# New orders for the four engines' lists of a layer kernel, one set each for the run-up, the steady bodies and the last four

## Chip, core and metric

One Trainium2 chip, one of its NeuronCores. The metric is the device time of one execution in microseconds (us), the median of the runs; lower is better.

## What is computed

Sixteen sequences of 512 tokens with 128 channels go through two layers. All arithmetic is float32 in meaning.

```python
x = x + chebyshev_attention(layernorm(x), W_in, W_out)       # 16 heads, causal running sums, orders 1 to 5
h = layernorm(x)                                             # the second layer normalises what it is given,
a = h + softmax_attention(layernorm(h) * g1 + b1)            # and normalises again inside: 16 heads of width 8, causal
a = a + moe(layernorm(a) * g2 + b2)                          # 8 experts of hidden width 512, top 2 for each token, erf gelu
return x + a
```

## The kernel before

The first phase is a software pipeline over the 16 sequences. `pipelined` (L327) calls `body` 21 times, with t from -5 to 15. Each body works on up to six sequences at once, each in another stage, and a stage whose sequence does not exist is None:

- f = t+5: first normalisation, projections, the Chebyshev powers of q and k;
- h = t+4: head sums, running sums, denominators, first output, residual, second pair of normalisations;
- g = t+3: projections of the softmax attention, the split of q and k into three bf16 parts, and their way through memory (`spread`) into the stack of rows that TensorE contracts over;
- m = t+2: for each query the maximum of its scores, in 44 tiles (`maximum`);
- b = t+1: scores again, with the maxima as two more rows of the stack, in 48 tiles (`scores`), exponentials (`exps`), values (`values`), normalisation of the output;
- t: second output, residual, third normalisation, gate, ranks, and `dispatch` of the tokens to the experts' regions by indirect DMAs.

So five bodies fill the pipeline (t = -5 to -1), twelve are full or nearly so (t = 0 to 11, with f None in the last), and four empty it (t = 12 to 15, where f and h are None and g runs in the first only). The second phase is the expert computation in 39 blocks and the sum of the pairs; neither its code nor its order is touched.

What sets the order: every engine takes its instructions strictly in the order in which the body issues them, and waits at its head for semaphores. For PE, DVE and ACT the body is a loop over 129 places, `for n in range(SLOTS)`; tables say at which places the many small tiles go (MAX_PE, SCORES_PE, VALUES_PE, MAX_DVE, EXPS_ACT, LEAVE_ACT), and `at(place, stage)` puts each other step at one place. One order serves all 21 bodies. POOL's body is plain code without places.

The steps that the prediction uses:

- `put_maxima(m, p, half)` (L974) issues on ACT's queue two DMAs of 8 KB that write the negated maxima of eight heads as two rows into the stack of scores of the coming body. `scores` number 0 of the next body waits for half 0 (`max_dma`, L1425 and after), number 24 for half 1.
- The stack reload (L392) is on SP's queue: two DMAs of 400 and 384 KB for each half of the heads. Half 0 may start once the spread is written and `scores` 24 of the body are done, half 1 once all 48 are done.
- `turn_maxima` (PE, L1406), `max_parts` (ACT, L972) and `max_rest` (DVE, L604) turn and split the maxima ahead of `put_maxima`.
- `turn_back`, `normalise`, `turn_y` and `take_y` (L994) end the body's attention; `output2` (PE, L1477) of the next body multiplies it, and `x2` (DVE, L621) adds the residual.
- `head_sums` (PE, L1320), ten matmuls each for k and q, need both powers of `fifth_order` (DVE, L536) and those of `even_orders` (POOL, L1153, L1154). `sum_k` (L553) and `den_terms` (L564) on DVE follow them.
- `ln_rsqrt` (POOL, L447 to L473) is a chain of small instructions; in its long form, for "m", it releases `apply1` and `apply2` (ACT, L480) and by them the next normalisation's turn.
- `less_first_part` (POOL, L1183) waits for the first bf16 parts that ACT writes in `take_qk` step 2 (L932, L934).
- `dispatch` (POOL, L1197) sends one tile of 128 tokens; there are eight for each sequence. For t = 12 to 14 it waits for the ones before, after each pair.

Of the kernel before, what the change touches and what calls it, by code (L numbers as in the profile page):

```python
# [28 lines left out]
B, T = 16, 512  # L29
QT = T // P  # L30
# [105 lines left out]
def block_kernel(nc, x, consts, cols, row_biases, w_in, w_out, wq, wk, wv, wp, gate_w, ew1, ew2, eb2, out):  # L136
    with ExitStack() as ctx:
# [87 lines left out]
        for c in "amb":  # L225
# [82 lines left out]
        SLOTS = 129  # L308

        MAX_PE = (0, 1, 5, 9, 12, 19, 21, 30, 31, 36, 44, 49, 51, 53, 56, 60, 62, 64, 67, 68, 70, 73, 75, 77, 81, 84, 86, 88, 91, 93,  # L310
                  95, 98, 100, 102, 106, 109, 112, 116, 118, 120, 121, 123, 124, 126)
        SCORES_PE = (2, 7, 8, 10, 11, 13, 14, 16, 17, 18, 20, 22, 24, 25, 27, 28, 32, 33, 35, 37, 40, 41, 46, 48, 50, 54, 55, 61, 66, 71,
                     72, 76, 82, 83, 87, 89, 92, 94, 97, 99, 104, 105, 108, 110, 111, 113, 115, 117)
        VALUES_PE = (15, 23, 26, 34, 43, 59, 78, 85, 101, 107, 119, 122)
        MAX_DVE = (1, 3, 5, 9, 11, 14, 15, 18, 23, 25, 27, 28, 29, 31, 32, 34, 35, 36, 38, 39, 40, 41, 44, 45, 49, 50, 53, 54, 56, 57,
                   58, 61, 62, 64, 66, 68, 69, 70, 71, 73, 74, 75, 76, 78)
        EXPS_ACT = (1, 3, 4, 5, 6, 7, 8, 9, 10, 11, 12, 13, 15, 16, 17, 18, 20, 21, 23, 24, 26, 28, 30, 35, 36, 39, 41, 44, 45, 49, 50,
                    52, 57, 59, 61, 62, 64, 65, 70, 71, 74, 76, 77, 78, 79, 80, 81, 82)
        LEAVE_ACT = (19, 42, 73)
        SPLIT_DVE, SPLIT_ACT = (8, 21, 52, 55), (0, 2, 32, 58, 60, 66, 72, 75)  # L320
# [15 lines left out]
        def _(sp):  # L336
# [28 lines left out]
            def body(t, b, m, g, h, f, p):  # L365
# [118 lines left out]
        def _(dve):  # L484
# [199 lines left out]
            def body(t, b, m, g, h, f, p):  # L684

                for n in range(SLOTS):
                    at = lambda place, stage: n == place and stage is not None
                    if b is None and t is not None and n in SPLIT_DVE:
                        second_weights(SPLIT_DVE.index(n))
                    if m is not None and n in MAX_DVE:  # L690
                        maximum(m, MAX_DVE.index(n))
                    if at(0, f):
                        stats0(f)
                        if f == 0:
                            set_tables()
                    if at(2, t):
                        x2(t)
                    if at(4, h):
                        sum_k(h)
                    if at(6, h):  # L700
                        den_terms(h)
                    if at(7, t):
                        stats3(t)
                    if at(10, h):
                        times_v(h, (0, 1))
                    if at(12, h):
                        sum_kv(h, (0,))
                    if at(13, h):
                        sum_kv(h, (1,))
                    if at(16, h):  # L710
                        times_v(h, (2, 3))
                    if at(17, h):
                        sum_kv(h, (2,))
                    if at(19, h):
                        times_v(h, (4,))
                    if at(20, h):
                        sum_kv(h, (3,))
                    if at(22, h):
                        sum_kv(h, (4,))
                    if at(24, h):  # L720
                        invert_den(h)
                    if at(26, t):
                        gate_top(t)
                    if at(30, t):
                        gate_weights(t)
                    if at(33, t):
                        slots(t)
                    if at(37, b):
                        normalise(b, 0)
                    if at(42, f):  # L730
                        clip(f, kx, W.hk_ev, W.k_clip)
                    if at(43, g):
                        third_part(g, 2, kf, ks)
                    if at(46, g):
                        third_part(g, 1, qf, qs)
                    if at(47, m):
                        max_rest(m, 0)
                    if at(48, f):
                        clip(f, qx, W.hq_ev, W.q_clip)
                    if at(51, f):  # L740
                        third_order(f, kx, W.k_sq, W.k_t35)
                    if at(59, b):
                        normalise(b, 1)
                    if at(60, h):
                        ratio(h)
                    if at(63, f):
                        third_order(f, qx, W.q_sq, W.q_t35)
                    if at(65, h):
                        add_x1(h)
                    if at(67, h):  # L750
                        stats1(h)
                    if at(72, b):
                        normalise(b, 2)
                    if at(77, b):
                        normalise(b, 3)
                    if at(79, f):
                        fifth_order(f, qx, W.q_sq, W.q_t35)
                    if at(80, f):
                        fifth_order(f, kx, W.k_sq, W.k_t35)
                    if at(81, m):  # L760
# [103 lines left out]
        def _(act):  # L864
# [151 lines left out]
            def body(t, b, m, g, h, f, p):  # L1016

                for n in range(SLOTS):
                    at = lambda place, stage: n == place and stage is not None
                    if b is None and t is not None and n in SPLIT_ACT:  # L1020
                        first_weights(SPLIT_ACT.index(n))
                    if b is not None and n in EXPS_ACT:
                        exps(b, EXPS_ACT.index(n))
                    if b is not None and n in LEAVE_ACT:
                        evacuate(b, LEAVE_ACT.index(n))
                    if at(14, t):
                        apply3(t)
                    if at(22, t):
                        affine2(t)
                    if at(25, f):  # L1030
# [616 lines left out]
```

## Time and profile before

| | us |
|---|---|
| median of 3 runs | 1379.57 (1373.16 to 1382.08) |
| the profiled execution | 1373.93 |
| its span, first to last instruction | 1372.1 |
| run-up, t = -5 to -1 | 0 to 210 |
| bodies t = 0 to 10 (eleven of them) | 210 to 836 |
| t = 11 to 15 | 836 to 1060 |
| experts and sum of pairs | 1060 to 1372 |

The borders are the times at which the first `scores` tile of a body starts, and for the second phase about the last dispatch. In the profile, "busy" is the time in which an engine ran instructions; PE's ends are modelled. "PEclk" is the granted clock of TensorE as a share of 2.4 GHz: 1.00 is 2.4 GHz and 0.50 is 1.2 GHz.

### The profile page before, as it was taken

Reading aid. Unit: us, or ns where it says so; the run is one execution under the profiler, and the core shown is the slowest. Engines: PE = TensorE matmul, PEld = TensorE weight load, DVE = VectorE, ACT = ScalarE, POOL = GpSimd, SP = SyncE. Lnnn points to the kernel's source line nnn. Section 1 sums busy time; section 2 is a strip of 40 time slices with the busy share of each in tenths; the row PEclk is TensorE's granted clock in tenths of the full one; section 3 lists DMA queues with packets and bytes.
Section 4 is the critical chain, followed back from the end, with each engine's and each line's share of the span. In section 5 each row is a group of like instructions: output and inputs, shape, how many; then the busy total and the mean of one; then the engine's idle time right before and its main releaser. Section 6 shows DMA issues by size and latency. Waiting matters only on the chain.

```text
span 1372.1 us, 27932 instructions
## 1 busy us (share of the span) xinstructions
PE 1141.6 (83%) x8883; PEld 702.2 (51%) x8883; DVE 1086.1 (79%) x2555; ACT 934.1 (68%) x1859; POOL 841.7 (61%) x1105
## 2 busy tenths in 40 slices
PE   3546898998989989889898998988893799999960
PEld 1223354454644546445464454544452588888840
DVE  4557888898988989899898897965715688888845
ACT  2334487696876968769687695675574699999940
POOL 2775566776877767777777686532224166666660
PEclk9677799999999999999999999988985899999985
DMA  9231231423324223142241422413232222222239
GB/s 207 50 88 51 49 88 30 109 72 60 97 51 105 72 58 101 31 115 78 58 103 41 96 77 44 104 62 73 84 127 104 78 79 85 84 86 82 67 139 367
DMA packets 84436, 121.91 MB, mean 89 GB/s; under 512 B 15270, under 2 KB 66522, under 8 KB 80002
## 3 DMA queue, kind: packets, MB, share of 16 engines
q1 hardware_dynamic: 70978, 98.07, 27.5%
q0 software_dynamic: 9088, 17.33, 3.6%
q10 hardware_dynamic: 4224, 4.72, 1.1%
q8 instruction: 71, 1.16, 0.4%
q14 instruction: 75, 0.61, 0.2%
HBM read 63.96 MB, written 57.46 MB: 88 GB/s over the span
## 4 chain that ended last, share of the span: by engine, by line
PE 65%; DMA 12%; DVE 10%; ACT 7%; issue 5%; POOL 1%; ACTq 1%; SPq 0%; POOLq 0%; DVEq 0%
PE back L1452 8%; PE front L1586 8%; PE back L1598 8%; DMA stack<-nms 7%; PE scores L1433 6%; PE front L1320 6%; PE maxima L1393 5%; ACT pr L986 4%; DVE nm L599 3%; PE scores L1435 3%; PE front L1295 3%; PE maxima L1395 3%; PE back L1270 2%; DMA stack<-pairs 2%; PE front L1477 1%
## 5 line engine op out<-in xcount | busy, mean ns | idle before, releaser
L986 ACT ACTIVATE pr<-scores 128x384 f32<-128x384 f32 (+1 forms) x768 | 369.6, 523 | 144.1 <-PE scores L1435 137.3
L599 DVE TENSOR_REDUCE nm<-maxima 128x1 f32<-128x384 f32 (+3 forms) x704 | 420.5, 631 | 44.4 <-PE maxima L1395 38.4
L1433 PE MATMUL scores<-stack 65*128 65x384 bf16 (+2 forms) x768 | 205.6, 285 | 57.3 <-DMA stack<-nms 32.6
L1393 PE MATMUL maxima<-stack 65*128 65x128 bf16 (+2 forms) x768 | 197.7, 282 | 16.2 <-DVE nm L599 14.5
L1197 POOL DMA_INDIRECT xg<-rows,sloti x128 | 137.0, 1070 | 108.0 <-DVE sloti L669 44.0
L1395 PE MATMUL maxima<-stack 128*128 128x128 bf16 x1024 | 182.6, 224 | 6.7 <-DMA stack<-spread 5.1
L1435 PE MATMUL scores<-stack 128*128 128x128 bf16 x1024 | 181.3, 225 | 0.0
L1452 PE MATMUL back<-pr,vaug 128*9 128x512 f32 (+3 forms) x2048 | 178.4, 444 | 1.5 <-ACT oT L990 1.0
L1433 PEld LDWEIGHTS scores<-stack 65*128 65x128 bf16 x768 | 75.6, 98 | 179.3 <-ACT pr L986 106.8
L1259 POOL DMA_INDIRECT pairs<-xs x104 | 111.0, 1068 | 78.7 <-DVE xs L832 51.9
L1393 PEld LDWEIGHTS maxima<-stack 65*128 65x128 bf16 x768 | 74.7, 98 | 121.9 <-DVE nm L599 87.4
L1586 PE MATMUL front<-h_first,w_now 128*128 128x512 f32 x312 | 126.2, 405 | 2.7 <-DVE h_second L812 2.5
L1127 ACT ACTIVATE xs<-front,b1p 128x512 f32<-128x512 f32 x156 | 107.5, 689 | 18.8 <-PE front L1586 16.6
L1162 POOL TENSOR_TENSOR kv<-F,kv 128x512 f32<-128x512 f32 x80 | 100.6, 1283 | 27.6 <-DVE kv L553 27.6
L1395 PEld LDWEIGHTS maxima<-stack 128*128 128x128 bf16 x1024 | 94.5, 100 | 29.9 <-issue 22.0
L1598 PE MATMUL back<-hid_first,w_now 128*128 128x512 f32 x312 | 96.3, 390 | 0.0
L1435 PEld LDWEIGHTS scores<-stack 128*128 128x128 bf16 x1024 | 92.4, 100 | 5.8 <-issue 4.6
L553 DVE TENSOR_TENSOR_SCAN kv<-one,front 128x512 f32<-128x512 f32 x80 | 93.7, 1204 | 0.0
L1320 PE MATMUL front<-F,cst 128*32 128x512 f32 x320 | 81.9, 804 | 3.9 <-DVE F L536 3.5
L1173 POOL TENSOR_TENSOR kv<-kv 128x512 f32<-128x512 f32 x64 | 80.4, 1267 | 2.4
L1153 POOL TENSOR_SCALAR F<-F 128x512 f32<-128x512 f32 x32 | 48.2, 1507 | 53.6 <-DVE F L532 53.3
L825 DVE TENSOR_TENSOR hid_second<-xs,hid_first 128x512 fp32r<-128x512 f32 x99 | 68.0, 687 | 15.7 <-ACT hid_first L1108 14.9
(219 smaller groups left out, 2459.5 us busy)
## 6 DMA issues: line engine op xcount, KB each, us to landing
stack<-spread SPq DMA_DIRECT2D x32, 400.0 KB
spread<-qs SPq DMA_DIRECT2D x96, 128.0 KB
spread<-ks SPq DMA_DIRECT2D x96, 128.0 KB
stack<-spread SPq DMA_DIRECT2D x32, 384.0 KB
xs<-xg SPq DMA_DIRECT2D x39, 272.0 KB, 2.9
stack<-pairs SPq DMA_DIRECT2D x8, 1024.0 KB, 13.5
stack<-in_consts SPq DMA_DIRECT2D x4, 1280.0 KB
xg<-xs SPq DMA_DIRECT2D x17, 272.0 KB
```

Of the source, the lines that this page charges most:

```text
L599: v.tensor_reduce(nm[:, h:h + heads, t], ring(n)[:, 0:heads * (t + 1) * P].rearrange("p (h n) -> p h n", h=heads), AX.X, ALU.max, negate=T ...
L986: a.activation(pr[:, n % PR, 0:width], ringE[n % 2][:, 0:width], ACT.Exp).then_inc(W.exp_ready, 1)
L1197: g_.indirect_dma_start(xg[:, :], bass.IndirectOffsetOnAxis(sloti[:, i, q:q + 1], 0), rows[:, i, q, :], None).then_inc(W.dispatched, 16)
L1259: g_.indirect_dma_start(pairs[:, :], bass.IndirectOffsetOnAxis(xt[i % XT][:, at:at + 1].bitcast(U32), 0), yo[i % 3][:, q * D:(q + 1) * D], ...
L1320: last = k.matmul(dst[32 * j:32 * j + 32, :], cst[:, C_SUM + 32 * var:C_SUM + 32 * var + 32], z[p], start=(p < 4), stop=(p > 0), skip_grou ...
L1393: k.matmul(ring(n)[:, at:at + t * P], qst[p][0:OPEN_ROWS, h, own], kst[p][0:OPEN_ROWS, h, 0:t * P], start=(j == 0), stop=True, skip_group_ ...
L1395: last = k.matmul(ring(n)[:, at + t * P:at + (t + 1) * P], qst[p][:, h, own], kst[p][:, h, own], start=(j == 0 and t == 0), stop=True, ski ...
L1433: k.matmul(dst[:, at + P:at + T - t * P], kst[p][0:OPEN_ROWS, h, own], qst[p][0:OPEN_ROWS, h, (t + 1) * P:T], start=(t == tiles[0]), stop= ...
L1435: last = k.matmul(dst[:, at:at + P], kst[p][:, h, own], qst[p][:, h, own], start=False, stop=True, skip_group_check=True)
L1452: last = k.matmul(V[32 * i:32 * i + DH + 1, t * P:T], vaug[:, b % VR, t, 4 * (s_ // 3) + i, :], pr[:, (4 * s_ + i) % PR, at:at + T - t * P ...
L1586: last = k.matmul((X, Y)[n % 2][:, :], w_now[:, i % 2, wi, c * P:(c + 1) * P], h2p[hi][:, i % 2, :], start=(j == 0), stop=(j == len(TERMS3 ...
L1598: last = k.matmul((Z, V)[i % 2][:, :], w_now[:, i % 2, 2 + wi, c * P:(c + 1) * P], (hidh, hidl)[hi][i % 2 * HC + c], start=(c == 0 and j = ...
```

## The change

Each step's single place becomes three, one each for the run-up, the steady bodies and the last four, and `body` is given `w` to choose. POOL gets a list of 25 places. One wait is added: `turn_ln` now waits also for `x2`, which reads the same PSUM bank.

```diff
 for t in range(-5, B):
-    body(*(t + i if 0 <= t + i < B else None for i in range(6)), (t + 1) % 2)
+    body(*(...), (t + 1) % 2, (t >= 0) + (t >= 12))

 # every body
-    at = lambda place, stage: n == place and stage is not None
+    at = lambda places, stage: n == places[w] and stage is not None

 # ACT
-if at(83, m):
+if at((77, 75, 70), m):
     put_maxima(m, p, 0)
-if at(38, g):
+if at((39, 41, 43), g):
     take_qk(g, 2)
-if at(22, t):
+if at((18, 16, 20), t):
     affine2(t)
-if at(34, t):
+if at((8, 36, 30), t):
     gate_exp(t)
 # unmoved in the steady bodies: put_maxima(m, p, 1) at 88, apply2 at 89

 # PE
-if at(4, h): head_sums(h, kx, ...)
-if at(6, h): head_sums(h, qx, ...)
+if at((0, 4, 66), h): head_sums(h, kx, ...)
+if at((2, 5, 17), h): head_sums(h, qx, ...)
-if at(47, g): project_k2(g)
-if at(52, g): project_q2(g, h)
+if at((47, 50, 59), g): project_q2(g, h)
+if at((41, 55, 44), g): project_k2(g)
-if at(58, t): ranks(t)
+if at((37, 60, 50), t): ranks(t)
-if at(127, b): turn_y(b)
-if at(128, m): turn_maxima(m, b, 1)
+if at((128, 127, 128), m): turn_maxima(m, b, 1)
+if at((127, 128, 127), b): turn_y(b)
-MAX_PE = (0, 1, 5, 9, 12, ...)
-SCORES_PE = (2, 7, 8, 10, 11, 13, ...)
+MAX_PE = ((6, 12, 14, ...), (1, 2, 12, 20, ...), (1, 2, 4, 7, ...))
+SCORES_PE = ((1, 3, 4, ...), (0, 6, 7, 8, 9, ...), (0, 6, 8, 9, ...))

 # DVE
-if at(0, f): stats0(f)
-if at(2, t): x2(t)
-if at(4, h): sum_k(h)
-if at(6, h): den_terms(h)
-if at(7, t): stats3(t)
+if at((68, 2, 3), t): x2(t)
+if at((81, 3, 5), t): stats3(t)
+if at((1, 4, 81), h): sum_k(h)
+if at((0, 5, 7), f): stats0(f)
+if at((2, 7, 15), h): den_terms(h)
-if at(46, g): third_part(g, 1, qf, qs)
+if at((47, 51, 60), g): third_part(g, 1, qf, qs)
-if at(80, f): fifth_order(f, kx, ...)
+if at((51, 80, 19), f): fifth_order(f, kx, ...)
-MAX_DVE = (1, 3, 5, 9, ...)
+MAX_DVE = ((8, 9, 10, ...), (0, 1, 12, 13, ...), (0, 2, 4, ...))

 # POOL, steady bodies: before
-add_residual, ln_rsqrt b, times_q 0, ln_rsqrt a, times_q 1 to 4, add_products (0, 1), less_first_part 0, 1,
-add_products (2, 3), dispatch x3, even_orders k, dispatch x3, even_orders q, ln_rsqrt m, dispatch x2, keep_residual
 # and after
+ln_rsqrt b, add_residual, ln_rsqrt a, times_q 0 to 4, add_products (0, 1), less_first_part 0, add_products (2, 3),
+less_first_part 1, dispatch x6, even_orders k, dispatch x2, even_orders q, ln_rsqrt m, keep_residual

 # PE
-def turn_ln(g, h):
+def turn_ln(g, h, t):
     pe.wait_ge(norm["m"]["out"], g * 8 + 8)
+    if t is not None:
+        pe.wait_ge(W.x2_ready, t + 1)
```

`SPLIT_DVE` and `SPLIT_ACT`, the places in body t = 15 at which the experts' weights are split, move from (8, 21, 52, 55) and (0, 2, 32, ...) to (20, 36, 45, 52) and (17, 24, 58, ...). The other places change by a few, as in the lines above.

## Rows read from the trace of the kernel before

**Rows 1.** The page: busy time, share of the span and instructions of each engine.

```profile
PE 1141.6 (83%) x8883; PEld 702.2 (51%) x8883; DVE 1086.1 (79%) x2555; ACT 934.1 (68%) x1859; POOL 841.7 (61%) x1105
```

**Rows 2.** Windows by body: length, busy (count) of PE, PEld, DVE, ACT, POOL; PEclk, DMA share, GB/s.

```profile
382.00:437.00 55.00, 50.66 (x473) 28.74 (x473) 50.79 (x130) 43.01 (x93) 42.85 (x59) 1.00 0.33 79
...
552.00:611.00 59.00, 53.93 (x475) 29.95 (x476) 51.68 (x130) 43.60 (x95) 43.07 (x60) 0.95 0.31 74
```

**Rows 3.** The chain that ended last, at the border into t = 6: start, us, what.

```profile
544.85 7.17 DMA stack<-nms
552.07 0.50 PE scores L1433
...
552.67 1.81 PE front L1477 x8
554.49 3.55 PE front L1320 x10
...
558.37 1.83 PE front L1320 x10
```

**Rows 4.** Timeline of PE at the border into t = 3: start, us, instruction [idle before <-releaser].

```profile
381.99 0.34 PE L1433 MATMUL scores<-stack 65*128 65x384 bf16 x1 [2.27 <-DMA stack<-nms]
...
385.43 1.90 PE L1320 MATMUL front<-F,cst 128*32 128x512 f32 x10
```

**Rows 5.** Waits in the eleven steady bodies: total us, times, longest.

```profile
PE scores L1433 <- DMA stack<-nms: 24.4, 11, 2.7
```

**Rows 6.** Timeline of ACT at the border into t = 6 and near the end of t = 6.

```profile
549.82 0.57 ACT L994 ACTIVATE hn<-back 128x512 f32<-128x512 f32 x1
...
552.20 1.65 ACT L480 ACTIVATE ha<-xs,morem 128x128 f32<-128x128 f32 x4 [1.80 <-POOL morem L473]
553.75 0.57 ACT L986 ACTIVATE pr<-scores 128x512 f32<-128x512 f32 x1
...
599.99 2.97 ACT L986 ACTIVATE pr<-scores 128x384 f32<-128x384 f32 x6 [0.78 <-PE scores L1435]
```

**Rows 7.** Windows of 1 us at the end of t = 6: ACT busy, PEclk, DMA share, GB/s.

```profile
600.00:601.00 1.00, 0.97 (x3) 1.00 0.04 13
...
605.00:606.00 1.00, 0.77 (x2) 1.00 1.38 239
```

**Rows 8.** DMA issues: KB each and median us from issue to landing.

```profile
gw_sb<-in_gate_w SPq DMA_DIRECT2D x1, 4.0 KB, 2.0
```

**Rows 9.** Timeline of POOL through t = 6.

```profile
544.07 0.22 POOL L447 TENSOR_SCALAR lnvm<-mvm 128x4 f32<-128x4 f32 x1
...
551.97 0.20 POOL L473 TENSOR_TENSOR morem<-morem 128x4 f32<-128x4 f32 x1
...
581.02 1.17 POOL L1183 TENSOR_TENSOR qf<-qf,qs 128x512 f32<-128x512 f32 x1 [1.62 <-ACT qs L932]
...
592.26 1.51 POOL L1153 TENSOR_SCALAR F<-F 128x512 f32<-128x512 f32 x1 [1.52 <-DVE F L532]
...
596.78 0.96 POOL L1197 DMA_INDIRECT xg<-rows,sloti  x1 [0.30 <-issue]
...
602.06 0.22 POOL L447 TENSOR_SCALAR lnvm<-mvm 128x4 f32<-128x4 f32 x1
```

**Rows 10.** Timeline of DVE and PE in the run-up, into t = -3 and t = -2.

```profile
56.97 0.69 DVE L584 TENSOR_TENSOR xs<-front,xs 128x512 f32<-128x512 f32 x1 [1.57 <-PE front L1355]
...
59.03 1.26 DVE L536 SCALAR_TENSOR_TENSOR F<-F 128x512 f32<-128x512 f32 x2
...
60.44 6.54 PE L1320 MATMUL front<-F,cst 128*32 128x512 f32 x20 [3.51 <-DVE F L536]
...
102.26 3.62 PE L1320 MATMUL front<-F,cst 128*32 128x512 f32 x10
```

**Rows 11.** Timelines of ACT and POOL in t = 14.

```profile
1013.28 0.20 ACT L1003 ACTIVATE gt<-gt 128x4 f32<-128x4 f32 x1
...
1016.97 1.10 POOL L1197 DMA_INDIRECT xg<-rows,sloti  x1 [16.38 <-DVE sloti L669]
```

More of the change, by code:

```diff
@@ L738, in body @@
[L738 to L742, printed above, removed]
[L743 to L748 removed]
+                    if at((39, 43, 53), g):
+                        third_part(g, 2, kf, ks)
@@ new lines, in body @@
+            def body(t, b, m, g, h, f, p, w):
+                for n in range(POOL_SLOTS):
+                    at = lambda places, stage: n == places[w] and stage is not None
+                    if at((20, 0, 3), t):
+                        ln_rsqrt("b", t)
+                    if at((1, 1, 2), t):
+                        add_residual(t)
+                    if at((2, 2, 22), f):
+                        ln_rsqrt("a", f)
+                    if at((3, 3, 9), h):
+                        times_q(h, (0,))
+                    if at((5, 4, 21), h):
+                        times_q(h, (1,))
+                    if at((8, 5, 13), h):
+                        times_q(h, (2,))
+                    if at((10, 6, 6), h):
+                        times_q(h, (3,))
+                    if at((15, 7, 7), h):
+                        times_q(h, (4,))
+                    if at((14, 8, 23), h):
+                        add_products(h, (0, 1))
+                    if at((11, 9, 5), g):
+                        less_first_part(g, 0)
+                    if at((17, 10, 14), h):
+                        add_products(h, (2, 3))
+                    if at((13, 11, 8), g):
+                        less_first_part(g, 1)
+                    if at((4, 12, 4), t):
+                        dispatch(t, 0, (0,))
+                    if at((7, 13, 10), t):
+                        dispatch(t, 0, (1,))
+                    if at((6, 14, 11), t):
+                        dispatch(t, 0, (2,))
+                    if at((24, 15, 12), t):
+                        dispatch(t, 0, (3,))
+                    if at((0, 16, 15), t):
+                        dispatch(t, 1, (0,))
+                    if at((9, 17, 16), t):
+                        dispatch(t, 1, (1,))
+                    if at((19, 18, 1), f):
+                        even_orders(f, kx, W.k_t35, W.k_t24)
+                    if at((16, 19, 18), t):
+                        dispatch(t, 1, (2,))
+                    if at((12, 20, 19), t):
+                        dispatch(t, 1, (3,))
+                    if at((21, 21, 17), f):
+                        even_orders(f, qx, W.q_t35, W.q_t24)
+                    if at((22, 22, 20), h):
+                        ln_rsqrt("m", h)
+                    if at((23, 23, 0), h):
+                        keep_residual(h)
+                    if at((18, 24, 24), t):
+                        wait_apart(pool, W.dispatched, t * (16 * 2 * QT) + 16 * 2 * QT)
+                        pool.sem_inc(W.rows_free, 1)
```

314 lines of the change are left out of this document (141 added, 173 removed), and 20 rows, old and new, of tables (EXPS_ACT, MAX_DVE, MAX_PE, SCORES_PE).

## The prediction

> **What bounds the kernel now.** I read the page first, for shares: PE is busy 83% of the span, DVE 79%, ACT 68%, POOL 61% [rows 1]. No engine stands out, so the average says little. Cutting the span into bodies says more. A steady body is DVE 51 to 52 us busy and PE 50 to 54, in 55 to 59 us [rows 2]. Two engines are near full, and what is left over is 4 to 7 us in each body. The reader should also see PEclk there: 1.00 in the 55 us body, 0.95 in the 59 us one. Of the twelve bodies from t = 0, three look like the first and nine like the second.
>
> Then the chain of waits, to see where those microseconds lie. At each border between bodies it leaves the engines: 7.17 us of DMA, the rows of the maxima of half 0, and only then the first scores tile of the new body [rows 3]. The waits confirm it: in eleven bodies PE stood 24.4 us before that tile, 2.2 each time [rows 5]. PE is in order, so the second output and the head sums, which need none of these rows, stand behind the tile. What follows runs slow as well: 3.55 us for ten head-sum matmuls that take 1.83 a few microseconds later, and 1.81 for the second output [rows 3]. Where the clock stays up, the whole set is over 5.34 us after the wait (381.99 to 387.33) against 8.13 in the slow case (552.07 to 560.20) [rows 3, 4].
>
> What releases the DMA late: it is issued behind the last exponential of the body, in the moment in which SP issues the reload of half 1. The DMA engines have nothing to do just before, a share of 0.04 at 600 us, and are flooded at 605 [rows 7].
>
> **The change, part by part, for a steady body.**
>
> *The rows of the maxima earlier (ACT place 83 to 75).* Seven exponentials now come behind them instead of none. The last six take 2.97 us from 599.99 [rows 6], so the issue moves some 4 us ahead, to about 599, into the gap of the DMA engines [rows 7]. How long they take alone no row shows: the nearest below is 2.0 us for a 4 KB load [rows 8], above 7.17 beside the reload [rows 3]. I take 3, near the small load, since the gap is empty: landed at 602. Even with 7.17 they land at 606, two microseconds before PE wants them at about 608, so this term holds over the whole bound. Price on ACT: two issues, some 1.1 us, now between two exponentials. The 0.78 us in which ACT waits for PE there [rows 6] hide most of it. Taken at nothing; without that cover it is 1.1 x 12 = 13 us.
>
> *What is late next at the border.* The second output needs take_y, which ended at 550.39 [rows 6]. From there: second output 0.95, two scores and maxima tiles 0.4, head sums 2 x 1.83 at the full clock, so done at 555.4 instead of 560.2, 4.8 us earlier. By the same sum at the fast border 2.2 earlier. Over twelve borders 9 x 4.8 + 3 x 2.2 = 50 us, if nothing takes it back.
>
> *POOL takes some back.* Its list closes a loop. The long ln_rsqrt of h ends at 552.17 and releases apply2 and then the first exponential at 553.75 [rows 6, 9]. From there the body runs on to the first bf16 parts at 581.02, which is 28.9 us, and POOL's list from there to the start of the next ln_rsqrt takes 21.0 (to 602.06) and that one 8.1 (544.07 to 552.17) [rows 9]: 58.0 in all. After the change two dispatches (0.96 + 0.30 each [rows 9]) stand before ln_rsqrt instead of behind it, +2.5, and the wait of 1.5 us before even_orders goes, because six dispatches instead of three stand before it: 22.1 + 8.1 = 30.2. On the other side of the loop the 4.8 us of the border come off. But project_k2, which the parts need, moves from PE place 47 (and q from 52) to 55, with two more scores tiles and one more maximum ahead; at half a microsecond of exponential each (2.97 for six [rows 6]) that is +1. So the slow body becomes 58.0 + 1.0 + 1.0 - 4.8 = 55.2, the fast one about 54.8 by the same steps. The 1.0 on POOL lies on the path only in part, because keep_residual and add_residual no longer stand ahead of the norms, so I take 54 for all. The floor is DVE's 51.2 busy [rows 2]; with the 5% of gaps that it has in the middle of a body that is 53.
>
> *The clock.* At nine borders the granted clock went from its 2.4 GHz level to 1.2 GHz after PE's idle wait, and three times, with the same wait, it did not [rows 2 to 4]. The sum above has it stay up. The Trainium skill (TensorE: Matmul & The Clock Gate, "What's actually happening") says that the slow clock is the default and activity lifts it. By that rule a filled border keeps the fast one. The trace agrees as far as the full-clock middles of the bodies go; no row shows a filled border. Should it fall anyway, the price is 3.55 - 1.83 and 1.81 - 0.95, 2.6 us at each of nine borders.
>
> *x2's wait added to turn_ln.* In the steady bodies x2 is done some 20 us before; nothing.
>
> So 56.9 us a body (626 us for eleven) become 54: 12 x 2.9 = 35 us.
>
> **The run-up.** Head sums of k started at 60.44, released by fifth_order at 59.03, itself behind the statistics; the bank was free from x1 at 57.66 [rows 10]. The new place of fifth_order for k, 51 instead of 80, removes that: 2.7 us into t = -3. Into t = -2 the maxima stood ahead of the head sums and held them to 102.26 [rows 10]; they now come behind. By the same distance to x1 the sums start some 4.7 us earlier. These bodies are then bound by other things, DVE above all, so of the 7.4 and of the border into t = -1 I take 6, with 0 and 14 as ends.
>
> **The last four.** The borders into t = 13 and 14 have the same DMA wait with the slow clock behind it, 2 us and 1 to 2 us of slow matmuls: I take 3 each, 6. In t = 14 the gate's exponential at 1013.28 leads to the dispatch at 1016.97, for which POOL had waited 16.4 us [rows 11]; it now has 18 exponentials ahead instead of 23, 5 x 0.5 = 2.5, and ranks come eight places sooner. I take 4. The weight splits move behind the third normalisation of t = 15 and cost ACT 2.6 us that end before the second phase needs them: nothing. The second phase stays.
>
> **Sum.** 35 + 6 + 6 + 4 = 51 from the profiled execution's 1373.9: 1323. The median of the runs is 5.6 us above that execution and two of three are near the median. On its scale it is 1328; I say 1326.
>
> **Rivals.**
> - *The wait goes, half of the gain stays away.* The clock falls at the border all the same, 9 x 2.6 = 23, or POOL's loop stays at its full 55.2 (+14), with some of both at the ends: 1326 + 25 = 1351. For it: nine of twelve borders fell, and the gap before turn_y stays. Against: three did not fall even with 2.3 us of idling.
> - *The maxima land no earlier where it counts.* third_part of q moves from place 46 to 51 and less_first_part of k behind two additions, so the reload of half 0 slides into the 600 us gap and the rows arrive beside it, and this repeats at every border. Then only run-up and tail change: 1372 (-8). Against: 7.17 us from 599 is still in time.
> - *Slower: POOL's loop takes over.* This happens if the border's gain does not reach the bf16 parts, since the first exponential waits for apply2, so for POOL, while POOL's own part has grown from 29.1 to 30.2. The loop is slower than the 56.9 of now once the way from ln_rsqrt's end to the parts takes over 26.7 us; it took 28.9 in the slow body and I count on 25. At 28 it is 58.2, +1.3 x 12 = 16, and the last bodies inherit it: 1398. Against: in the old order head sums, not apply2, held the second exponential back by 6 us.
>
> **How the numbers follow.** Forecast 0.65, first rival 0.20, second 0.07, slower 0.08. The forecast's own range is 1300 (bodies of 53, run-up 12, tail 12) to 1345 (ACT's issues uncovered). The range with the first rival in it is 1296 to 1358. A per cent, 14 us, is about what this kernel's measurement can tell. The forecast and the first rival lie beyond it on the fast side: faster 0.84, same 0.08, slower 0.08.
>
> **What would show it.** In the profile after: no DMA step of the maxima in the chain at steady borders; PE's wait for them under 0.5 us each; steady bodies of about 54 us at PEclk 1.00, DVE 94 to 95% busy; head sums into t = -2 before the first maxima. Wrong: bodies above 56 with PEclk below 0.98, or POOL idle under 5 us a body with ACT waiting for L473.

## The result, and the profile after

The changed kernel takes 1336.4 us, median of four executions (1332.6 to 1343.8), beside 1379.0 us for the kernel before on the same chip: a ratio of 0.971, with a 95% interval of 0.966 to 0.975. The forecast was 1326, the range 1296 to 1358. The gain is 43 us where 53 were forecast, on the side that had been given 0.84.

The profiled execution of the changed kernel is the slowest of its four (1343.8 us, span 1342.0). The one of before was 5.6 us under its median. So the two traces differ by only 30 us, and what follows uses them for where the time lies, and the medians for how much it is. One execution of the kernel before on another chip (chip B below) took 2715.6 us and is left out everywhere.

The page's first part, with the same columns as [rows 1]:

```profile
PE 1131.7 (84%) x8883; PEld 706.3 (53%) x8883; DVE 1101.1 (82%) x2555; ACT 938.9 (70%) x1859; POOL 845.8 (63%) x1105
```

The counts are the same, so the instructions are the same and only their order moved. DVE's busy time still rose by 15 us; the section on the prediction comes back to that. Windows by body, with the columns of [rows 2]:

```profile
264.00:320.00 56.00, 52.65 (x465) 29.78 (x466) 51.16 (x128) 42.94 (x92) 42.07 (x60) 0.94 0.28 72
377.00:431.00 54.00, 50.37 (x474) 28.87 (x473) 51.52 (x129) 43.46 (x93) 42.57 (x60) 1.00 0.33 81
...
541.00:596.00 55.00, 51.04 (x478) 29.36 (x477) 52.48 (x130) 43.54 (x93) 42.29 (x60) 1.00 0.34 80
```

DVE is now busy for 51.2 to 52.5 us in 54 to 56. The granted clock is 1.00 in two of the three windows shown; over the eleven bodies t = 0 to 10 of this trace it is 1.00 in six and 0.94 to 0.97 in the others. Before, nine bodies of twelve fell [rows 2].

The border into t = 5 in PE's timeline. It corresponds to [rows 4], where PE stood 2.27 us for the maxima's rows:

```profile
484.42 0.22 PE L1430 MATMUL maxima<-stack 128*128 128x128 bf16 x1
484.84 1.16 PE L1512 MATMUL front<-wp_sb,hn 128*128 128x128 f32 x8 [0.21 <-ACT hn L1014]
485.93 3.62 PE L1353 MATMUL front<-F,cst 128*32 128x512 f32 x20
489.64 0.34 PE L1468 MATMUL scores<-stack 65*128 65x384 bf16 x1
```

The second output (L1512) and the twenty head sums (L1353) run at the full clock, without the wait, and before the first scores tile. In the list of waits the step "scores <- DMA stack<-nms" of [rows 5] (24.4 us) no longer occurs. The rows land in 3.3 us (all instructions on that tile, so both halves, last line of the answer; 208 to 820 us; half 0 alone 3.1 to 4.3):

```profile
DMA to landing us min/median/max: 1.9/3.3/4.3
```

What is late next stands in the chain of waits, here the end of t = 5 (start, us, what):

```profile
522.43 0.96 POOL xg L1217
523.70 0.95 POOL xg L1217
...
525.95 1.55 POOL F L1173
527.50 1.46 POOL F L1174
...
534.91 1.05 POOL lnvm L468
538.14 0.67 ACT hs L500 x2
...
539.94 0.49 ACT hn L1014
540.47 1.16 PE front L1512 x8
541.63 3.55 PE front L1353 x20
```

This end of the chain goes through POOL: its gathers (`xg`, the indirect DMAs of `dispatch`), even_orders, the norm's reciprocal root, then ACT and the head sums. That is POOL's loop from the prediction. POOL's waits over the steady bodies (208 to 819 us: total us, times, longest):

```profile
POOL qf L1203 <- ACT qs L952: 38.7, 11, 3.8
...
POOL xg L1217 <- ACT rows L1027: 14.7, 10, 3.1
```

The second line is new: POOL's gathers wait for ACT's copy of the rows, which moved from ACT place 29 to 49. ACT's waits in the same stretch:

```profile
ACT pr L1006 <- PE scores L1470: 48.4, 84, 1.7
ACT ha L500 <- POOL morem L493: 25.2, 11, 2.7
```

The last view is ACT's timeline at the new place of the first issue:

```profile
584.12 0.53 ACTq L997 DMA_DIRECT2D stack<-nms  x1
584.44 0.48 ACT L1006 ACTIVATE pr<-scores 128x384 f32<-128x384 f32 x1
584.68 1.93 ACTq L997 DMA_DIRECT2D stack<-nms  x1
586.72 2.41 ACT L1006 ACTIVATE pr<-scores 128x384 f32<-128x384 f32 x5 [1.79 <-issue]
```

The second of the two issues takes 1.93 us here, and the next exponential starts as it ends (584.68 + 1.93 = 586.61), after 1.79 us of idle time. This is the longest of eleven such places: the second issue of half 0 takes 0.95 to 1.93 us in them, with a median of 1.22, and ACT is idle for 0.81 to 1.79 us, with a median of 1.08.

Where the microseconds went is read from one mark per body, the start of the head sums of k. The first column is its time in t = -1, the second the twelve bodies from there to the mark in t = 11 (so t = -1 and the eleven steady bodies t = 0 to 10), the third what remains to the end of the span (the steady body t = 11, the last four and the second phase). The experiments of the next section stand in the same table. A to D are the chips on which the kernels ran, and the ratio is against the kernel before on the same chip.

| kernel | chip | to t = -1 | 12 bodies | rest | span | ratio |
|---|---|---|---|---|---|---|
| before | A | 155.3 | 683.1 | 533.7 | 1372.1 | 1 |
| changed | A | 151.2 | 667.7 | 523.1 | 1342.0 | 0.971 |
| before (c0_before) | B | 158.4 | 689.2 | 534.2 | 1381.7 | 1 |
| changed (c1_after) | B | 151.6 | 662.5 | 525.1 | 1339.2 | 0.972 |
| e5_steady_before | B | 151.4 | 659.5 | 523.9 | 1334.8 | 0.965 |
| e6_only_steady_new | B | 155.1 | 660.8 | 540.6 | 1356.5 | 0.983 |
| e1_put_early | C | 157.7 | 667.6 | 545.2 | 1370.5 | 0.968 |
| e2_put_late | C | 145.7 | 792.4 | 555.5 | 1493.6 | 1.051 |
| e3_copy_early | C | 151.3 | 711.8 | 543.9 | 1407.0 | 0.999 |
| e4_pool_before | C | 146.3 | 741.2 | 542.5 | 1430.0 | 1.018 |
| changed (c2_after) | D | 151.5 | 714.7 | 545.8 | 1412.0 | 0.998 |
| e7_put_early_again | D | 156.2 | 664.3 | 548.4 | 1368.9 | 0.972 |
| e8_copy_early_again | D | 151.2 | 711.8 | 540.9 | 1404.0 | 1.003 |
| e9_pool_before_again | D | 147.0 | 744.9 | 549.1 | 1441.0 | 1.020 |

On chip A the change wins 4 us before t = -1, 15 in the twelve bodies and 11 in the rest. On chip B both traces lie within 3 us of their medians, and there it is 7, 27 and 9, together 42.5, the whole gain. So the pair of B is the better guide to sizes. Over t = 0 to 10 alone a body goes from 56.9 us to 55.5 on A and from 57.5 to 55.0 on B. The second phase is untouched: from its first matmul to the end it takes 298.7 us before (from 1073.4) and 298.9 after (from 1043.1).

### The profile page after: what moved, and what is told of

Read it like the earlier page. It is cut to its first block, busy times and chain, and to the rows that moved or that the text cites. A ratio compares the mean times of both kernels' runs of the same rounds, so it can differ in the third digit from the quotient of the medians.

```text
span 1342.0 us, 27933 instructions
## 1 busy us (share of the span) xinstructions
PE 1131.7 (84%) x8883; PEld 706.3 (53%) x8883; DVE 1101.1 (82%) x2555; ACT 938.9 (70%) x1859; POOL 845.8 (63%) x1105
## 3 DMA queue, kind: packets, MB, share of 16 engines
q8 instruction: 71, 1.16, 0.4%
## 4 chain that ended last, share of the span: by engine, by line
PE 49%; DVE 17%; POOL 12%; issue 9%; ACT 8%; DMA 4%; POOLq 1%; ACTq 0%; SPq 0%; DVEq 0%
PE front L1621 8%; PE back L1633 8%; DVE nm L619 7%; PE back L1487 5%; POOL xg L1217 4%; PE scores L1468 4%; PE front L1353 4%; ACT pr L1006 3%; PE maxima L1428 3%; POOL F L1173 2%; PE scores L1470 2%; DMA stack<-pairs 2%; DVE front L570 2%; POOL F L1174 2%; PE maxima L1430 2%
## 5 line engine op out<-in xcount | busy, mean ns | idle before, releaser
L1006 ACT ACTIVATE pr<-scores 128x384 f32<-128x384 f32 (+1 forms) x768 | 373.5, 524 | 105.6 <-PE scores L1470 88.3
L1217 POOL DMA_INDIRECT xg<-rows,sloti x128 | 133.0, 1039 | 130.0 <-ACT rows L1027 43.4
L1182 POOL TENSOR_TENSOR kv<-F,kv 128x512 f32<-128x512 f32 x80 | 107.9, 1372 | 21.8 <-DVE kv L573 21.8
L1147 ACT ACTIVATE xs<-front,b1p 128x512 f32<-128x512 f32 x156 | 107.7, 690 | 18.6 <-PE front L1621 16.6
L1128 ACT ACTIVATE hid_first<-xs 128x512 fp32r<-128x512 f32 x117 | 74.1, 634 | 3.7
L1292 POOL DMA_INDIRECT pairs<-pr,xs x52 | 55.0, 1058 | 26.9 <-DVE pr L852 12.3
```

The costliest lines, as they stand in the source:

```text
L1006: a.activation(pr[:, n % PR, 0:width], ringE[n % 2][:, 0:width], ACT.Exp).then_inc(W.exp_ready, 1)
L1182: g_.tensor_tensor(kv[:, p, :], qx[p], kv[:, p, :], ALU.mult).then_inc(W.qk_prod, 1)
L1217: g_.indirect_dma_start(xg[:, :], bass.IndirectOffsetOnAxis(sloti[:, i, q:q + 1], 0), rows[:, i, q, :], None).then_inc(W.dispatched, 16)
L1292: g_.indirect_dma_start(pairs[:, :], bass.IndirectOffsetOnAxis(xt[i % XT][:, at:at + 1].bitcast(U32), 0), yo[i % 3][:, q * D:(q + 1) * D], ...
```

## The experiments

The theory: the first issue of the maxima's rows, moved ahead of the reload of half 1, is what gains in the steady bodies; the run-up and the last four gain a little of their own; POOL's loop takes the rest back. The rival: the new orders as a whole carry the gain, and the issue alone does little.

**e1_put_early, e7_put_early_again.** The kernel before with one number changed:

```diff
-                    if at(83, m):
+                    if at(75, m):
                         put_maxima(m, p, 0)
```

> The kernel before with one edit: the rows of the maxima of half 0 are issued at ACT place 75 instead of 83, in all bodies. If the gain is the wait at the border between bodies, PE's wait for these rows goes and most of the 42.6 us of the whole change comes with this edit alone: 1341 to 1356. If the new orders carry the gain and the early rows only permit it, this stays within 8 us of the kernel before: 1371 or more.

It took 1371.0 us beside 1415.9 for the kernel before: ratio 0.968 (0.965 to 0.971). Chip C was slower than chip A with the kernel before, so it was run again, on a fourth chip:

> The same kernel as the experiment with the early issue alone (the kernel before, with only the first issue of the maxima's rows moved from place 83 to 75), because that ran on a chip on which the kernel before took 1416 us. Theory (the early issue is the gain of the steady bodies; the rest of the change's gain is run-up and last four): about 1380 - 26 = 1354 us where before takes 1380, which lies between the kernel before and the changed one (1340). Rival (it is worth the whole change, as its ratio of 0.968 on the other chip says): 1337 us or less.

1372.2 beside 1409.5, ratio 0.972 (0.966 to 0.977). The microseconds of both my sentences were worked out for a chip on which before takes 1380, so they can't be held against this run. The ratio can: 0.972 of 1380 is 1341, nearer the rival's 1337 than the theory's 1354. On chips C and D the one moved issue is worth as much as the whole change is on A. This compares times alone, since the kernel before was not traced on C or D; e5 below makes the same comparison in traces of one chip. The twelve bodies of e7 are 55.4 us each (664.3 / 12), with PE and DVE busy for 93% of the stretch:

```profile
208.00:811.00 603.00, 560.15 (x5137) 313.91 (x5135) 558.40 (x1401) 470.48 (x1013) 462.48 (x633) 0.99 0.31 77
```

**e2_put_late.** The changed kernel with the issue back behind the last exponentials, all other orders new:

```diff
-                    if at((77, 75, 70), m):
+                    if at((83, 83, 82), m):
                         put_maxima(m, p, 0)
```

> The kernel after with the rows of half 0 issued behind the last exponentials again (places 83, 83, 82); all else stays. Border theory: PE waits 2 us and more for the rows at each of fourteen borders, with slow clock behind most, 1360 to 1380. If the orders carry it: under 1345. The two issues no longer stand between exponentials 40 and 41, where ACT idled 0.8 to 1.8 us, so if that is on the path some 1 us a body comes back, inside these numbers.

1489.1 us, ratio to before 1.051 (1.047 to 1.054), far more than the expected 1360 to 1380, even counting that chip C is slower; the changed kernel took 0.998 of before on chip D. D is close to C in every kernel that ran on both (before 1415.9 and 1409.5, the others 1371.0 and 1372.2, 1414.8 and 1415.0, 1438.1 and 1442.9 us). So the place of this issue is worth about 5% within the new orders, 78 us in the twelve bodies (792.4 against 714.7, on two chips). PE's waits in the steady bodies are back, and longer than in [rows 5]:

```profile
PE scores L1468 <- DMA stack<-nms: 33.0, 9, 3.8
```

and behind each of them the second output runs at half the speed, as in [rows 3] (PE's timeline at a border):

```profile
397.57 0.50 PE L1468 MATMUL scores<-stack 65*128 65x384 bf16 x1 [3.60 <-DMA stack<-nms]
...
398.83 2.02 PE L1512 MATMUL front<-wp_sb,hn 128*128 128x128 f32 x8
```

**e3_copy_early, e8_copy_early_again.** The changed kernel with ACT's copy of the rows back at its old place in the steady bodies. I had not priced this move in the prediction, and POOL's new wait of 14.7 us made it a suspect.

```diff
-                    if at((28, 49, 36), t):
+                    if at((28, 29, 36), t):
                         copy_rows(t)
```

> The kernel after with copy_rows at ACT place 29 instead of 49 in the steady bodies, as in the kernel before. In the trace after, POOL stands 14.7 us in eleven steady bodies before its first dispatch for copy_rows. If POOL's loop is what sets the body now, nearly all of it comes back: 1.0 to 1.3 us a body, 1321 to 1326. If DVE or the loop through the exponentials sets the body, nothing: 1333 to 1340.

1414.8 us, ratio 0.999 (0.997 to 1.002), which looks like a loss of 3% against the changed kernel of chip A. It isn't one; that took a second run beside the changed kernel:

> The same kernel as the copy_rows experiment (changed kernel, ACT copies the rows at place 29 again in the steady bodies). Theory: POOL's wait of 14 us for the rows goes, and turns into as much waiting of POOL for DVE's F tiles, so it equals the changed kernel within 5 us, and its 1415 us were the chip's: stalls of ACT and DVE that the trace put down to nothing in the kernel ('remote', 35 us together) and that the changed kernel's second trace doesn't have. Rival (the edit itself upsets ACT's list): 30 us or more slower than the changed kernel, with the same bodies of 58 to 62 us.

1415.0 us beside 1409.2 for the changed kernel (c2_after) on the same chip. Ratios to before 1.003 (1.000 to 1.006) and 0.998 (0.996 to 1.001): within half a per cent, a shade slower if anything. POOL's wait for the rows is gone and its wait for F is up from 32.5 us in the changed kernel on that chip to

```profile
POOL F L1173 <- DVE F L552: 47.8, 17, 4.0
```

So the suspect is cleared, on these chips; on A and B the edit was not tried. What POOL doesn't wait for at the gathers, it waits for at even_orders behind them. The 3% belong to the chip and the changed kernel together, as c2_after below shows.

**e4_pool_before, e9_pool_before_again.** The changed kernel with POOL's list of before in the steady bodies, the other three engines' lists new:

```diff
             def body(t, b, m, g, h, f, p, w):
+                if w == 1:
+                    if t is not None:
+                        add_residual(t)
+                        ln_rsqrt("b", t)
...
+                    return
                 for n in range(POOL_SLOTS):
```

> The kernel after with POOL's order of the kernel before in the steady bodies. My prediction priced the new order of POOL at about +1 us a body (two dispatches ahead of the long norm chain, less one wait): by that this kernel is 5 to 12 us faster, 1325 to 1331. If the early third normalisation and the order around less_first_part pay for more than that, it is slower: 1342 to 1355.

1438.1 us, 1.018 (1.014 to 1.022), and again with the changed kernel beside it:

> The same kernel as the experiment with POOL's order of before in the steady bodies beside the other three engines' new orders. Theory: POOL's old order puts the even orders of k after three gathers only, and copying the rows now comes late, so POOL waits for ACT's rows and DVE for F: steady bodies longer by 2 to 4 us, 1365 to 1390 us. Rival (only the slow chip made it 1438): equal to the changed kernel within 5 us.

1442.9 us against 1409.2: 2.4% slower, 30 us in the twelve bodies (744.9 against 714.7), 2.5 each, within the 2 to 4 expected. (The 1365 to 1390 us were worked out for a chip like A.) The changed kernel carries a stall of some 2.4 us in most of its bodies on this chip, described under c2_after, and e9 does not have it in t = 0 to 10, so the old list costs more than these 2.5 us. ACT's apply3 now waits 39.3 us for POOL's norm of t, which stands behind add_residual again, and POOL waits for DVE:

```profile
ACT rows L500 <- POOL moreb L491: 39.3, 9, 4.7
...
POOL F L1173 <- DVE F L552: 35.2, 10, 5.3
POOL kv L1182 <- DVE kv L573: 29.1, 19, 2.3
```

The lists belong together. POOL's new one is worth nothing by itself that I could show, but the other three don't run with the old one.

**c0_before and c1_after.** Both kernels unchanged, to learn what chip C does; they ran on chip B.

> The kernel before, unchanged, looked at on the chip that ran the first four experiments, where it took 1415.94 us against 1379 on the other one. If that chip is slower evenly, every steady body is some 2.7% longer (58.4 us instead of 56.9) with the same waits; if its DMA transfers or its instruction supply are slower, the difference sits in one kind of wait: landings of the maxima's rows above 7.2 us, or idle time that the trace puts down to nothing ('issue', 'remote').

> The changed kernel, unchanged, on the chip of the experiments. If the chip is slower by one factor, it takes 1336 x 1415.9 / 1379 = 1372 us, ratio 0.970; then copying the rows at place 29 cost 3% (42 us) and POOL's old order in the steady bodies 4.8% (66 us). Rival: the changed kernel suffers more from whatever slows this chip, as the 57.6 to 62.4 us bodies of the copy_rows experiment suggest: then it takes 1400 to 1415 here, and those two edits cost little or nothing.

Chip B is like chip A (before 1381.3; this execution 1383.6). The changed kernel took 1340.7, ratio 0.972 (0.965 to 0.978): the result of chip A again. What it would do on chip C, the actual question, stayed open; on D, which is close to C, the rival's 1400 to 1415 us came (c2_after). The profile of before on chip B repeats its wait, 24.4 us in all, and gives a number that [rows 3] could only show once, the landing of half 0 issued in the same moment as the reload:

```profile
DMA to landing us min/median/max: 5.9/6.8/8.0
```

**e5_steady_before.** The changed kernel, with all four lists of before in the twelve steady bodies and only the issue moved in them; run-up and last four as changed. The edit is the one of e4 for all four engines, with this in ACT's copy of the old list:

```diff
-                        if at(83, m):
+                        if at(75, m):
                             put_maxima(m, p, 0)
```

> The changed kernel with all four engines' orders of before in the twelve steady bodies, and only the first issue of the maxima's rows moved to place 75 in them; run-up and last four as changed. Theory (the early issue is the whole gain of the steady bodies, the new steady orders add nothing): steady bodies of 55.0 us as in the experiment with that one edit (1371 us), the run-up shorter by about 6 and the last four by about 8: 1357 us, ratio 0.958, not slower than the changed kernel. Rival (the new steady orders are worth their part, and the one edit alone only had luck on its chip): slower than the changed kernel on this chip by 10 us or more.

1330.7 us (1328.6 to 1336.7) beside 1340.7 (1335.1 to 1343.6) for the changed kernel on the same chip; ratios 0.965 (0.959 to 0.970) and 0.972 (0.965 to 0.978). The rival is out: the new steady orders gain nothing that the issue doesn't give alone. The theory's side, not slower, holds; by the medians it is 10 us faster, with intervals that overlap. (Its 1357 us were worked out from e1's time on the slower chip.) Within the steady bodies e5 differs from the kernel before by this one issue and by the wait added to turn_ln, and against c0_before on the same chip the twelve bodies gain 29.7 us (689.2 and 659.5), where the new lists gain 26.7. It is the fastest kernel of this study. The rows of half 0 land sooner:

```profile
DMA to landing us min/median/max: 1.9/2.2/3.2
```

The reload of half 0 is issued about 6 us before these rows in e5 and 4.0 us before them in the changed kernel, that of half 1 some 4 and 5.5 us behind them. In the microsecond of the first issue the DMA share is 0.39 to 0.61 in the eleven bodies of e5 and 0.78 to 1.14 in those of the changed kernel. The second issue takes 0.61 us in eight of e5's eleven bodies. That this is worth the 10 us is not shown.

**e6_only_steady_new.** The reverse: new lists in the steady bodies, the old ones, with the issue at place 83, in run-up and last four.

```diff
             def body(t, b, m, g, h, f, p, w):
+                if w != 1:
...
+                        if at(83, m):
+                            put_maxima(m, p, 0)
...
+                    return
```

> The changed kernel with the orders of before in the run-up and the last four bodies (the maxima's first rows at place 83 there), the new orders only in the twelve steady bodies. Theory: run-up and last four are worth about 4 and 11 us of the 43, so this is 15 us slower than the changed kernel (about 1387 us here, ratio 0.98). Rival: the stages gain nothing of their own (what the run-up wins is given back at its end), and it equals the changed kernel within 5 us.

1358.4 us, 17.7 slower than the changed kernel, where the theory said 15. By the table, 3.5 of it lie before t = -1 and 15.5 behind the mark in t = 11, more than the 9 to 11 that this part gains against the kernel before. That the old last bodies fit the new steady ones less well than their own would explain it; it was not tested.

**c2_after.** The changed kernel beside e7, e8 and e9, on chip D.

> The changed kernel once more, so that the other three of this call are compared on one chip. On a chip on which before takes 1380: 1340 us. On the one on which it takes 1416: 1372 if that chip slows all kernels alike, 1400 or more if it slows the changed one more; the first would leave the copy_rows and POOL experiments' losses as costs of their edits.

1409.2 us, ratio to before 0.998 (0.996 to 1.001). Here the change gains nothing, while one edit of it gains 2.8% (e7). Of the two cases in that sentence the second came: the chip slows the changed kernel more than the one before. So the losses of e3 and e4 against 0.971 are not the cost of their edits alone, as read above. The time is in the steady bodies, 59.7 us each (t = 0 to 10) against 55.0 on B, and a stall stands in nine of these eleven. ACT's timeline on chip B, then on chip D, at the same instructions:

```profile
299.16 0.63 ACT L917 ACTIVATE F<-F 128x512 f32<-128x512 f32 x1 [0.33 <-DVE F L547]
299.80 0.49 ACT L1006 ACTIVATE pr<-scores 128x384 f32<-128x384 f32 x1
300.18 0.71 ACT L922 ACTIVATE F<-F,negc 128x512 f32<-128x512 f32 x1
```

```profile
299.92 0.63 ACT L917 ACTIVATE F<-F 128x512 f32<-128x512 f32 x1 [0.29 <-issue]
302.99 0.49 ACT L1006 ACTIVATE pr<-scores 128x384 f32<-128x384 f32 x1 [2.44 <-remote]
303.38 0.71 ACT L922 ACTIVATE F<-F,negc 128x512 f32<-128x512 f32 x1
```

From 297 us to this point the two traces run 0.76 us apart, instruction by instruction. Then ACT stands 2.44 us, ended by nothing that the profile knows ("remote"), and DVE waits 1.15 us for a maximum of PE in the same stretch. The stall comes again at 363.78, 422.98, 483.42, 542.10, 602.70, 661.90, 722.35 and 842.78, always at this instruction, always of 2.44 to 2.49 us; the body around 782 us has none. So the stall itself makes some 22 of the 52 us that the twelve bodies are longer than on B. Some 5 us behind the first one PE's clock is down (windows of 1 us, PE alone: busy, PEclk, DMA share, GB/s):

```profile
302.00:303.00 1.00, 0.81 (x2) 1.00 0.20 70
303.00:304.00 1.00, 0.46 (x8) 1.00 0.05 17
...
307.00:308.00 1.00, 1.00 (x9) 1.00 0.62 115
308.00:309.00 1.00, 0.87 (x6) 0.75 0.90 279
309.00:310.00 1.00, 1.00 (x8) 0.50 1.19 180
```

On B the same windows are full and stay at 1.00. On D the clock stays at 0.50, its 1.2 GHz level, for some seven microseconds behind the thinned stretch (300 to 307 us), in which PE was busy for 0.44 to 0.81 of each microsecond.

Which kernels have the stall? On C and D those with POOL's new steady list do: e2, e3, e8 and c2_after show 6 to 9 of 2 us and more in t = 0 to 10, on ACT in front of an exponential, up to 4.1 us long. Those with the old list (e1, e7, e4, e9) show none there; e1 and e7 have only 0.8 us or less on DVE, at xs, in most bodies. On A and B no kernel has it. The new list puts six of POOL's gathers in a row across this stretch, the old one three.

One body separates the gathers from the rest of the list. In t = 11 there is no f, so the old list skips even_orders too, and six gathers stand in a row there as well. In just that body e1 has two stalls of 2 us and more on ACT (2.65 and 2.17 us) and so has e4 (2.91 and 2.44). The last of the six gathers and the two stalls, from e1:

```profile
862.74 0.96 POOL L1197 DMA_INDIRECT xg<-rows,sloti  x1 [0.30 <-issue]
```

```profile
860.50 0.27 ACT L972 ACTIVATE nms<-maxima 32x128 bf16<-32x128 f32 x1 [2.65 <-remote]
...
864.92 1.10 ACT L986 ACTIVATE pr<-scores 128x384 f32<-128x384 f32 x2 [2.17 <-remote]
```

That makes the six gathers in a row the strong candidate. It is still argued, not shown: of the other kernels on C and D only e3 has the stall on ACT in t = 11, though all have the six gathers there; no run changed the gathers alone, and what on the chip holds ACT back was not found. Nor was e5 tried on C or D.

## Why the prediction was right, and where it was not

**The border (4.8 us at slow ones, 2.2 at fast ones).** Right in its mechanism. The DMA step is gone from the waits, the head sums run as one set of 3.55 to 3.62 us, and the clock holds. e5 shows on one chip that this one issue gives the gain of the steady bodies, e1 and e7 agree, and e2 shows that taking it back costs more than all the change gained. The sum took 0.95 us for the second output at the full clock; it takes 1.11 to 1.16.

**The rows' landing (3 us taken, between 2.0 and 7.17).** 3.3 measured, 2.2 in e5. The size is right, but not for the reason given, that the gap is empty: in the changed kernel the reload of half 0 is issued 4.0 us before the rows, and the DMA share is 0.97 in the microsecond of the first issue at 584 us. The rows landed in time all the same. That the size came out so near is luck.

**The two issues on ACT (taken at nothing; 13 us if uncovered).** Somewhat mis-sized. The second takes 1.22 us (median of eleven) instead of 0.55, and ACT stands 1.08 us before the next exponential, where it stood 0.78 [rows 6]; in the worst body 1.93 and 1.79. That is 0.3 us more on ACT in a usual body, 1.0 in the worst. Whether any of it reached the end of a body was not tested.

**The length of a steady body (54: POOL's loop of 55.2, of which "the 1.0 on POOL lies on the path only in part, so I take 54 for all").** This is the term that was mis-sized. The steady bodies took 55.5 us on chip A and 55.0 on B (t = 0 to 10), near the loop's own sum, which the prediction had and then chose against. At 55.2 the twelve bodies give 12 x 1.7 = 20 us instead of 35, and the sum is 36 us instead of 51, which on the scale of the medians is 1343. The measured 1336 lies between that and the forecast. Single bodies did reach 54 (377 to 431 us).

That POOL's loop is what holds the body at 55 is read from the chain of one border, and no experiment isolated it. e5 speaks against it: it has POOL's old list and project_k2 at its old place, so the prediction's sum loses both of its 1.0 and gives 58.0 - 4.8 = 53.2, but its bodies took 54.8.

DVE is a rival that the prediction had only as a floor. The prediction gave its floor as 51.2 us busy, 53 with 5% of gaps (by that arithmetic it is nearer 54). In windows over t = 0 to 10 it is busy for 51.1 us a body before (562.6 / 11), but for 52.2 in the changed kernel on A and B (574.8 and 574.5 / 11) and 52.0 in e5 (571.9 / 11). With the idle share that it has there, 5 to 6%, that is the body: 55.5, 55.0 and 54.8. Its waits for the second output and the head sums of k, 17.8 and 17.5 us over eleven bodies before, are down to 2.9 and nothing, so there was little left to take. In the changed kernel most of the rise is in two kinds of instruction that only take longer at their new moments. One is shown, before and after (208 to 820 us; busy us, mean ns); the other, `front<-F,va`, went from 691 to 772 ns over 55 of them:

```profile
L665 DVE TENSOR_TENSOR oh<-oh,slot 128x64 f32<-128x64 f32 x11 | 3.4, 306 | 0.0
```

```profile
L685 DVE TENSOR_TENSOR oh<-oh,slot 128x64 f32<-128x64 f32 x11 | 11.5, 1049 | 0.0
```

What lengthens them was not tested, and which of the two, DVE or POOL's loop, holds the body stays open.

**A move that was missed.** The copy of the rows, ACT place 29 to 49, was not in the sum, though it moved much further than the "few" places that the section on the change speaks of. It made a new wait of 14.7 us on POOL. It cost nothing that e8 could show, because the wait for F stands right behind it. The sum escaped this error by luck, not by its working.

**The clock ("the sum above has it stay up").** It stayed up over the filled borders, and at 1.00 through six of eleven steady bodies on A and eight on B. Where PE's work was thin it fell: at the border into t = 1, where the second output took 2.08 us behind an idle wait of 1.63 for ACT, in e2 behind its wait, and on chip D behind the stall. On B the same wait of 1.63 left it up (1.16 us). The rule cited from the Trainium skill (TensorE: Matmul & The Clock Gate, "What's actually happening"), that activity lifts the clock, agrees with what filled borders show here.

**The run-up (6, with 0 and 14 as ends).** 4 us on A, 7 on B, to t = -1. On A the sums into t = -2 did start 6.7 us earlier (95.6 for 102.3), but the next body gave 2.6 of it back. The direction and the places were right, the amount near.

**The last four (6 + 4).** The third column of the table, 10.6 us on A and 9.1 on B, also holds the steady body t = 11. Counted from the second output of t = 12 to the end it is 8.8 us on A (478.0 and 469.3) and 6.7 on B (477.8 and 471.1): right in kind, a little short of 10.

**The rivals.** The first (half of the gain stays away, 1351) named bodies of 55.2, and that length is what came, without the fall of the clock: the result lies between forecast and rival, somewhat nearer the forecast. The second (rows land no earlier) came in its first half only: the reload of half 0 did slide to just before the rows, but they landed in 3.3 us all the same. The slower one (POOL's loop over 56.9) did not come on A or B. On C and D the changed kernel and its close kin have bodies of 59.5 us and more, those of c2_after are 59.7, but through a stall that no reasoning of mine contained, not through that loop.

**Where the rest of the forecast went.** The parts forecast were 6, 35 and 10 us. Cut at the second outputs of t = 0 and t = 12, so that the middle part is the twelve steady bodies, the pair of traces on B gives 5.3, 30.5 and 6.7, the pair on A 2.7, 18.6 and 8.8. On B, where the pair shows the whole gain, 4.5 of the missing 8.5 us lie in the steady bodies, 0.7 in the run-up and 3.3 in the last four. The bodies of before are 57.5 us there and not 56.9, which hides a part of what 54 was too short by.

## What to carry to other kernels

Where an in-order engine waits for a small DMA, look at what the queues do as it is issued, and move that issue away from the moment of a large transfer's issue before touching anything else: in the steady bodies one number gave what four new lists gave. When a prediction sums a loop that closes through a third engine, take the sum unless a row shows a way around it, and take the busy time of the fullest engine as a term that can grow by a new order, not as a constant. And run such a schedule on more than one chip before keeping it: new orders that gained 3% on two chips gained nothing on a third, where the plain edit still did.

## What was unexpected of the hardware

Chips differ, and not by a factor. The kernel before took 1379 and 1381 us on A and B, 1416 and 1409 on C and D. The changed kernel took 1336, 1341 and, on D, 1409. The kernel with the one edit took 1371 and 1372 on C and D, in bodies of 55.8 and 55.5 us (t = 0 to 10), about as short as the changed kernel's on A. They are 0.7 to 1.0 us longer than the 54.8 of e5 on B, which has the same steady lists and the same early issue; e1 and e7 idle 0.74 to 0.78 us at one DVE instruction in most of these bodies ("remote"). The second phase is longer there too: 307.6 us from its first matmul in e7 and 309.5 in c2_after, against 299.1 in c1_after. Why the kernel before is slower on C and D no trace shows.

The stall on chip D is as regular as an instruction, 2.44 to 2.49 us at one place in nine of eleven bodies of the changed kernel, with DVE and PE thinned beside it. It appears where six gathers stand in a row on POOL, even under the old list. What it is stays open.

The same DVE instruction on a tile of 128 x 64 took 306 ns in one order and 1049 in another, each a mean of eleven.

The issue of a DMA on ACT has no fixed price. The same instruction took 0.51 to 1.93 us in one trace, with a median of 0.57 (208 to 820 us):

```profile
L997 ACTq DMA_DIRECT2D stack<-nms x46: 510/568/1932, 207.9 to 818.2; - x46
```
